# A fifteenth slab slot in a GNN and mixture kernel, and a rule in place of a table for the slot of each mixture load

## What is computed

```python
x = x + gnn_l(layernorm(x))        # attention over the edges, one or two layers, l = 0..3
x = x + ffn_l(layernorm(x))        # l = 0: attention and a small MLP, l = 2: 8 small experts
# l = 1 and l = 3: a mixture of 8 experts, 2 of them chosen for each row
out = sum over experts e of c[:, e] * ((silu(x @ Wg[e].T) * (x @ Wu[e].T)) @ Wd[e].T)
```

## Time and profile before

| | us |
|---|---|
| median of three runs | 1215.71 (1215.35 to 1215.76) |
| the profiled execution, its own time | 1215.62 |
| its span, first to last instruction | 1213.8 |
| PE busy | 1147.2 (95%) |
| VectorE busy | 564.9 (47%) |
| ScalarE busy | 446.8 (37%) |
| data moved | 443.13 MB, mean 365 GB/s |

### The profile page before, as it was taken

The page is one execution under the profiler, slowest core; times in us unless marked ns, Lnnn a source line. Parts: engine busy times, 40 slices in busy tenths (PEclk is TensorE's granted clock), DMA queues, the critical chain, the costliest instruction groups (busy, mean ns, idle before and its releaser), DMA issues.

```text
span 1213.8 us, 15596 instructions
## 1 busy us (share of the span) xinstructions
PE 1147.2 (95%) x6307; PEld 717.6 (59%) x6307; DVE 564.9 (47%) x880; ACT 446.8 (37%) x516; POOL 21.9 (2%) x47
## 2 busy tenths in 40 slices
PE   5899999989999999989999999999999999889978
PEld 4677785656855455535866686565665555445533
DVE  6977732437644234301665684454554533233310
ACT  4766512224633233201444364343544422222210
POOL 2000000000000000000000000000000000000000
PEclk9999999999999999999999999999999999899999
DMA  9998555945999999999567498999999999999996
GB/s 371 423 374 339 218 221 211 422 169 229 386 419 425 424 426 426 424 421 417 222 234 268 192 390 327 426 425 425 425 427 424 426 424 425 426 425 425 426 423 273
DMA packets 45222, 443.13 MB, mean 365 GB/s; under 512 B 5072, under 2 KB 5232, under 8 KB 11872
## 3 DMA queue, kind: packets, MB, share of 16 engines
q1 hardware_dynamic: 42336, 427.05, 85.0%
q0 software_dynamic: 2816, 15.09, 3.2%
HBM read 441.73 MB, written 0.39 MB: 364 GB/s over the span
## 4 chain that ended last, share of the span: by engine, by line
PE 75%; DMA 14%; DVE 6%; ACT 4%; issue 1%; SPq 0%; POOL 0%; DVEq 0%; ACTq 0%
PE PJ L1896 15%; PE PJ L1865 10%; PE TP L1955 8%; DMA scratch<-in_weights 7%; PE AC L1933 7%; DMA ring<-in_weights 6%; PE PJ L1874 5%; PE AC L1681 3%; PE AC L1693 3%; PE PJ L1856 2%; PE TP L1906 2%; PE MS L1528 2%; PE PJ L1641 1%; PE TP L1824 1%; DVE extra L1058 1%
## 5 line engine op out<-in xcount | busy, mean ns | idle before, releaser
L1896 PE MATMUL PJ<-scratch,picked 128*64 128x512 f32 (+1 forms) x564 | 145.9, 600 | 3.8 <-DMA scratch<-in_weights 3.8
L1955 PE MATMUL TP<-ring,extra 128*64 128x512 f32 (+3 forms) x720 | 118.0, 488 | 3.5 <-issue 3.5
L851 ACT ACTIVATE low<-PJ 128x512 f32<-128x512 f32 x51 | 30.3, 593 | 231.5 <-PE PJ L1896 158.9
L1292 DVE SCALAR_TENSOR_TENSOR act<-low,CB,PJ 128x512 f32<-128x512 f32 x51 | 38.0, 745 | 164.2 <-PE PJ L1865 84.1
L1310 DVE TENSOR_TENSOR ring_lo<-ring,w_hi_u 128x1536 fp32r<-128x1536 f32 x46 | 79.6, 1756 | 69.7 <-ACT w_hi_u L868 69.6
L1896 PE MATMUL PJ<-ring,picked 128*32 128x512 f32 (+1 forms) x456 | 101.6, 594 | 0.0
L868 ACT ACTIVATE w_hi_u<-ring 128x1536 fp32r<-128x1536 f32 x46 | 67.0, 1485 | 57.2 <-PE AC L1933 26.9
L1310 DVE TENSOR_TENSOR ring_lo<-ring,w_lo_u 128x1536 fp32r<-128x1536 f32 x40 | 68.9, 1755 | 37.9 <-ACT w_lo_u L868 37.8
L1955 PEld LDWEIGHTS TP<-ring,extra 128*64 128x64 f32 (+1 forms) x720 | 47.1, 126 | 63.0 <-issue 54.7
L1874 PE MATMUL PJ<-ring_lo,XTh 128*128 128x512 f32 x198 | 79.0, 399 | 0.0
L1896 PEld LDWEIGHTS PJ<-scratch,picked 128*64 128x64 f32 (+1 forms) x564 | 42.4, 126 | 60.4 <-issue 59.7
(11 more groups left out here) (439 smaller groups left out, 2099.6 us busy)
## 6 DMA issues: line engine op xcount, KB each, us to landing
ring<-in_weights SPq DMA_DIRECT2D x158, 1536.0 KB, 17.8
scratch<-in_weights SPq DMA_DIRECT2D x78, 1536.0 KB, 20.7
extra<-in_weights SPq DMA_DIRECT2D x23, 1536.0 KB, 20.7
extra<-in_attn POOLq DMA_DIRECT2D x11, 768.0 KB, 9.8
ring<-in_weights SPq DMA_DIRECT2D x10, 768.0 KB, 29.9
scratch<-in_weights SPq DMA_DIRECT2D x12, 384.0 KB, 16.6
extra<-in_attn POOLq DMA_DIRECT2D x6, 512.0 KB, 9.7
extra<-in_weights SPq DMA_DIRECT2D x4, 768.0 KB, 26.0
```

What stands on the lines that cost most here:

```text
L851: A(silu, PJ[:, 0:SEG], ACT.Silu).then_inc(S("silu_ready"), 1)
L1292: v.scalar_tensor_tensor(hexp, silu, weight, PJ[:, SEG:2 * SEG], ALU.mult, ALU.mult) \
L1896: ins = mm(dst[c], x[:, t, c], slab_at(LOAD[q, kind, side])[:, t * SEG:(t + 1) * SEG], start=(t == 0), stop=(t == KT - 1))
L1955: ins = mm(Y[c, a:b], hT_of(q)[:, t * P:(t + 1) * P][:, c], slab_at(LOAD[q, "d", side])[:, t * D + a:t * D + b], start=(j == j0 and t == 0 ...
```

## The change

A fifteenth slot, number 14, is added as a fourth plane of `extra`. Its 12,288 bytes in every partition come from the scratch of POOL's DMA descriptors, for which the program now asks 2048 bytes (before it asked for nothing, and the library's default is 16,384). The two tables go. `uses_of` lists the order in which a mixture's products run, and `slots_in_turn` gives each load the slot whose slab has the earliest last use; the tokens' slot 13 enters that list with the place at which the tokens are used up, and slot 12 is not used behind load 70 of the first mixture. The first mixture so has 13 slots, the second 12, and nine slots take slabs 117 to 126. The small tiles of the GNNs of layers 1 and 3 are laid closer together, inside slot 6 alone, so that slot 7 is free for its first mixture load at an earlier event.

```diff
-TURN = {
-    1: [0, 1, 8, 9, 2, 3, 4, 13, 5, 7, 12, 6],
-    3: [8, 9, 2, 3, 4, 5, 0, 1, 7, 12, 6],
-}
-OPENING = {
-    1: [0, 1, 8, 9, 2, 3, 4, 5, 6, 7, 12],
-    3: [8, 9, 2, 3, 4, 5, 0, 1, 6, 7, 12],
-}
...
-free = [SLOT[n] for n in range(L2_SLAB - len(TURN[1]), L2_SLAB) if SLOT[n] in QUIET]
+RING_SLOTS, SPLIT_SLOTS = range(0, 6), range(6, 12)
+EXTRA_AT = {12: 0, 13: 1, 14: 3}
+N_SLOTS = 15
+QUIET = [0, 1, 2, 3, 4, 5, 8, 9, 14]
+TOKENS_SLOT = 13
+VECTORS_SLOT, VECTORS_SLOT_UNTIL = 12, 70
+
+def uses_of(l):
+
+    first, end = MOE[l]["first"], LAST_PASS[l] + 1
+    order = [(kind, p) for q in range(first, end + 1) for kind, p in (("g", q), ("u", q), ("d", q - 1))]
+    return {(p, kind, side): at for at, (kind, p) in enumerate(order) if first <= p < end for side in range(sides(p))}
+
+def slots_in_turn(l, opening):
+
+    uses = uses_of(l)
+    given_up = {s: k - len(opening) for k, s in enumerate(opening)}
+    if l == 1:
+        given_up[TOKENS_SLOT] = uses[MOE[1]["first"] + 1, "d", 0] + 0.5
+    taken = []
+    for k, load in enumerate(loads_of(l)):
+        s = min((s for s in given_up if s != VECTORS_SLOT or l != 1 or k < VECTORS_SLOT_UNTIL), key=given_up.get)
+        given_up[s] = uses[load]
+        taken.append(s)
+    return taken
+
+SLOT = {n: n % RING for n in range(MOE[1]["slab"])}
+for k, s in enumerate(slots_in_turn(1, [14, 7, 0, 1, 8, 9, 2, 3, 4, 6, 5, 12])):
+    SLOT[MOE[1]["slab"] + k] = s
...
 for k in range(10):
-    SLOT[L2_SLAB + k] = free[k % 8]
+    SLOT[L2_SLAB + k] = free[k % 9]
+for k, s in enumerate(slots_in_turn(3, [7, *free[1:8], 6, free[8], free[0], 12])):
+    SLOT[MOE[3]["slab"] + k] = s
...
-        with nc.sbuf_tensor("extra", [P, 3, SLAB], F32) as extra:
+        with nc.sbuf_tensor("extra", [P, 4, SLAB], F32) as extra:
...
-                        if SLOT[n] in (6, 7):
+                        if SLOT[n] == 6:
                             sp.wait_ge(S("segment_product"), segments)
+                        if SLOT[n] == 7:
+                            sp.wait_ge(S("context" if l == 1 else "x_product"), {1: 1, 3: 4}[l])
...
-    nc = bacc.Bacc("TRN2", target_bir_lowering=False, num_devices=1)
+    nc = bacc.Bacc("TRN2", target_bir_lowering=False, num_devices=1, dynamic_dma_scratch_size=2048)
```

More of the change, by code:

```diff
@@ L140 @@
         LOAD[load] = MOE[l]["slab"] + k
-RING_SLOTS, SPLIT_SLOTS, EXTRA_SLOTS = range(0, 6), range(6, 12), range(12, 14)
-HI_SLOTS = (10, 11)
-TURN = {
-    1: [0, 1, 8, 9, 2, 3, 4, 13, 5, 7, 12, 6],
-    3: [8, 9, 2, 3, 4, 5, 0, 1, 7, 12, 6],
-}
-OPENING = {
-    1: [0, 1, 8, 9, 2, 3, 4, 5, 6, 7, 12],
-    3: [8, 9, 2, 3, 4, 5, 0, 1, 6, 7, 12],
-}
[L155 to L168, removed]
-free = [SLOT[n] for n in range(L2_SLAB - len(TURN[1]), L2_SLAB) if SLOT[n] in QUIET]
+RING_SLOTS, SPLIT_SLOTS = range(0, 6), range(6, 12)
[22 more added lines that the diff above has]
+    SLOT[MOE[1]["slab"] + k] = s
+free = []
+for n in range(L2_SLAB - 1, MOE[1]["slab"], -1):
+    if SLOT[n] in QUIET and SLOT[n] not in free:
+        free.insert(0, SLOT[n])
 for k in range(10):
-    SLOT[L2_SLAB + k] = free[k % 8]
+    SLOT[L2_SLAB + k] = free[k % 9]
+for k, s in enumerate(slots_in_turn(3, [7, *free[1:8], 6, free[8], free[0], 12])):
+    SLOT[MOE[3]["slab"] + k] = s
 HI = {}
@@ L299, in gnn_ffn_kernel @@
         ring_lo = sb("ring_lo", [P, RING, SLAB], F32R)
-        with nc.sbuf_tensor("extra", [P, 3, SLAB], F32) as extra:
+        with nc.sbuf_tensor("extra", [P, 4, SLAB], F32) as extra:
             pass
-        extra_lo = sb("extra_lo", [P, 3, SLAB], F32R)
+        extra_lo = sb("extra_lo", [P, 4, SLAB], F32R)
         at = [0]
@@ L396, in gnn_ffn_kernel @@
         ALT = carve(3 * SEG)
+        narrow = {
+            2: (hs1[:, 0:2 * SEG], hs1[:, 2 * SEG:4 * SEG], hs1[:, 4 * SEG:6 * SEG]),
+            5: (hs1[:, 0:4 * SEG], hs1[:, 4 * SEG:4 * SEG + 3 * P], hs1[:, 4 * SEG + 3 * P:4 * SEG + 6 * P]),
+        }
         end[0] = H_RING * SEG
@@ L441, in slab_at @@
                 return scratch[:, (s - RING) * SLAB:(s - RING + 1) * SLAB]
-            return extra[:, s - 2 * RING, :]
+            return extra[:, EXTRA_AT[s], :]
         def slab_lo(n):
@@ L450, in slab_lo @@
                 return (wh if s % 2 == 0 else wl)["dgu"[(s - RING) // 2]][:]
-            return extra_lo[:, s - 2 * RING, :]
+            return extra_lo[:, EXTRA_AT[s], :]
         def graph_hi(s, half):
@@ L481, in gnn_ffn_kernel @@
         Y = TP[:, SEG:SEG + D]
-        land = [S(f"slab_landed_{i}") for i in range(14)]
+        land = [S(f"slab_landed_{i}") for i in range(N_SLOTS)]
         def landed(eng, n):
@@ L502, in group, with group_at, h_tile @@
             n = min(k, GAT[c]["H"] - g * k)
-            at = (g % 3) * SEG
+            at = group_at(c, g)
             return GROUP_BASE[c] + g, n, slice(at, at + n * P)
+        def group_at(c, g):
+            return (g % 3) * (P if c == 5 else SEG)
+        def h_tile(c, j):
+            return narrow[c][0][:, j * SEG:(j + 1) * SEG] if c in narrow else hs1[:, ring_seg(j)]
         def logit_tile(c):
-            return low[0] if c in LAYER2_BIAS else EE
+            return low[0] if c in LAYER2_BIAS else narrow[c][1] if c in narrow else EE
         def attn_tile(c):
-            return low[1] if c in LAYER2_BIAS else ALT
+            return low[1] if c in LAYER2_BIAS else narrow[c][2] if c in narrow else ALT
         def rows_tile(c, g):
@@ L719, in copy_h @@
                 act.wait_ge(S(name), value)
-                A(hs1[:, ring_seg(j)], bank(j), ACT.Copy).then_inc(S("h_copied"), 1)
+                A(h_tile(c, j), bank(j), ACT.Copy).then_inc(S("h_copied"), 1)
             def copy_h2():
@@ L1232, in first_narrow @@
                         dve.wait_ge(S("h_copied"), SEG_BASE[c] + t + 1)
-                        terms(GAT[c]["unit"] + t, range(t * k, t * k + k), C, hs1[:, ring_seg(t)])
+                        terms(GAT[c]["unit"] + t, range(t * k, t * k + k), C, h_tile(c, t))
                         if c == 5 and t == 0:
@@ L1638, in attend @@
                     g = h // GAT[c]["group"]
-                    a = (g % 3) * SEG + (h % GAT[c]["group"]) * P
+                    a = group_at(c, g) + (h % GAT[c]["group"]) * P
                     o = at - i * SEG
-                    ins = mm(bank(i)[:, o:o + end - at], ALT[:, a:a + P],
-                             hs1[:, (i % H_RING) * SEG + o:(i % H_RING) * SEG + o + end - at],
+                    ins = mm(bank(i)[:, o:o + end - at], attn_tile(c)[:, a:a + P], h_tile(c, i)[:, o:o + end - at],
                              start=False, stop=(end == (i + 1) * SEG), skip_group_check=True)
```

## The result

The changed kernel takes **1208.45 us** (median of 4 runs, 1207.72 to 1209.44) beside 1215.74 us before (1215.35 to 1216.71). The ratio is 0.994 [0.9927, 0.9953]: 7.3 us less, with an interval of 5.7 to 8.9 us. Timed again on two chips, beside the kernel before on each, it gave 0.9947 [0.993, 0.9965] and 0.9943 [0.9925, 0.9961]. The forecast was 1209.3 us, faster.

What follows compares the result with a forecast made beforehand. Both mixtures were taken as races of the load queue, at 3.70 us a slab. Gains of 2.7 us in the first and 3.7 us in the second made 6.4 us, forecasting 1209.3 us, range 1207.0 to 1212.0 us.

Steps and rivals of the forecast that it cites:

- Term 1: First mixture, 320 to 324 us: loading slabs ahead of the tokens' wait closes the queue's hole, 2.7 us (0 to 3.7).
- behind 345 us the queue is full already: First mixture: the reason given why the added slot brings nothing there beyond the hole's 2.7 us.
- Term 2: Second mixture: one slot more gives one slab's lead at the last dry release, 747.84 us, worth 3.7 us (0 to 5.0).
- from there on the queue is full in both kernels: Second mixture, behind the release at 747.84 us: the lead of one slab, 3.7 us, is kept to the end.
- Sum: Whole kernel: 2.7 + 3.7 = 6.4 us off the profiled 1215.62 us, giving a median of 1209.3 us.
- Passing on: Between the mixtures: the first's 2.7 us arrive whole at the second's first routed load, 690.35 us moving to about 687.7.
- PE's idle time at the two ends: Ends of both mixtures: a sign that PE's idle time shrinks by about 3 and 4 us.
- Loads at nothing, and the scratch at nothing: Loads needing no routing and POOL's smaller descriptor scratch cost nothing; at worst one slab, 3.7 us, and 9.8 us respectively.
- the holes did not close altogether: Rival, both mixtures: releases come earlier too and all holes close, 13.4 us, 1202.3 us; chance 0.05, with any gain over 9 us.
- neither gain came alone: Rival, both mixtures: only one of the two gains comes, 1212.0 or 1213.0 us; chance 0.08.
- the slot was not spent ahead of the gate: Rival: the fifteenth slot takes a slab needing no routing and buys nothing behind it, 1215.7 us; chance of no effect 0.06.
- `rstd` came at 5.39 us: Rival at POOL's start: short scratch holds its second vector load 9.8 us, `rstd` later than 6 us, 1219.1 us; chance 0.05.

Runs made afterwards that it cites:

- the order alone: The changed kernel with slot 14 unused in both mixtures, so fourteen slots in the give-up order, timed against the kernel before: 1216.14 us, ratio 1.0001.
- the slot without the order: The changed kernel with its fifteen slots going round in a fixed circle instead of the give-up order, timed against the kernel before: 1217.79 us, ratio 1.002.
- one pass more ahead: The changed kernel with AHEAD 4 instead of 3, so twelve slabs of the second mixture need no routing: 1210.99 us, 0.996 against the kernel before.
- the scratch alone: The kernel before with only POOL's descriptor scratch cut from 16,384 to 2048 bytes: 1215.69 us, ratio 0.9996.

## Why the prediction was right, and where its terms were off

- **What bounds the kernel**: right. Both mixtures are races of the queue; what the queue gains behind its last dry moment arrives at the end. The time from end 1 to gate 2 has no trend with the change (125.2 to 129.2 us over all kernels), so the gain is passed on.
- **Term 1, the hole of the first mixture, 2.7 us (0 to 3.7)**: mis-sized. It measured 4.1 us (277.5 to 273.4, the means of the kernels with fourteen slots and of those with the slot here), a little over the upper bound. Two steps failed. The term was put down to the order of the waits, the slot being said to add nothing in the first mixture: the kernel with the order alone gains nothing that the timing shows, the slot without the order nothing either. It takes both, and together they give the lead that the argument reserved for the second mixture. And the step "behind 345 us the queue is full already" left the stretch from 324 to 345 us unread. Between 330 and 345 us the kernel before runs at 411 GB/s and loses another 0.5 us, so 3.2 us with the hole. The last 1.0 us is not in the data moved: by the mean of its sixteen marks the mixture's last strip comes 3.1 us earlier, and the last mark then stands 1.3 us behind that mean instead of 2.2 (five profiles of each kind, with the closing strips as in the changed kernel). That the marks lie closer together with the slot is shown, its cause is not. The same is seen in landings: slabs 53 and 54 lie 5.7 us apart before and 3.7 after, and from 54 to 62 it takes 31.9 us before and 29.6 after, 2.0 + 2.3 us.
- **Term 2, a slab's lead in the second mixture, 3.7 us (0 to 5.0)**: right in its mechanism, and 0.6 us too large: 3.1 us from gate 2 to slab 264 (493.0 to 489.9, means over the kernels with fourteen slots or with the circle, and over those with slot 14 here; the kernel with one pass more ahead is left out). The step that failed is "from there on the queue is full in both kernels": the 8 us behind the dry stretch run at 378 GB/s instead of 413 and give 0.7 us back. The rest of the dry stretch stayed, as stated: 352 GB/s. The 1.3 us that were counted as lost from 690.5 to 716 us, and put into the upper bound, are mostly the time from the first issue to its first data: from 691.44 to 716.94 us the same kernel moves 415 GB/s.
- **Sum**: 4.1 + 3.1 = 7.2 us against the 6.4 predicted and the 7.3 [5.7, 8.9] measured. That the sum came out so near is partly luck, since the two errors lean against each other. The profiled execution shows only 6.2 us: its closing strips took 1.5 us longer and gate 1 came 0.4 us later, and 0.8 us came back behind the last landing.
- **Passing on**: gate 2 was put at 687.7 us and came at 686.41, mostly by term 1's error.
- **PE's idle time at the two ends**, put at 3 and 4 us less: 63.00 - 58.61 = 4.4 us in the 63 us up to the end of the first mixture (the stretch 496.50 to 559.50; 8.4 before), so 4.0 less; 306.00 - 289.42 = 16.6 us in the second (18.7 before), 2.1 less.
- **Loads at nothing, and the scratch at nothing**: right. The first routed load of the first mixture went 0.36 us later in the first profile (285.98 us) and at 285.65 and 285.59 us in the other two, and the scratch alone is at 0.9996. SP's queue is no shorter with the small scratch: before and with the scratch alone, every load of SP whose issue takes over 1.2 us finds nine to twelve loads in flight. The Trainium skill (DMA: Bandwidth & Descriptors, SWDGE vs HWDGE vs iDMA), by which the prediction weighed this, says that descriptors of SP's loads are made by hardware, and these figures agree; no run here shows the rings themselves.
- **Rivals**: the holes did not close altogether; neither gain came alone; the slot was not spent ahead of the gate; `rstd` came at 5.39 us.

## What to carry to other kernels

Where a stream of loads waits for room in a ring of buffers, look for the last moment at which it does. In this kernel a buffer more was worth about one transfer there (4.1 and 3.1 us; a transfer is 3.7 us), however full or empty the stream was elsewhere, and filling idle time ahead of that moment only moved the idle time. The buffer paid only where the transfer that takes it waits for the product that comes first: a load that waits for a later one holds everything behind it in an in-order queue, and a fixed circle with one buffer more gained nothing (1.002). When a hole is to be closed, read the stretch behind it too: closing it by order alone moved it some 10 us on, and behind the second mixture's dry stretch part of the lead was lost again.

## What the runs showed of the hardware that was not expected

An issue of SP takes 0.33 us as a rule, and up to 7.37 us in the changed kernel with nine or more loads in flight (the step on SP's line of strips in the chain above), so near the end SP's issues themselves appear on the chain. A load's sixteen landing marks do not come together: those of slab 62 spread over 3.0 us before and 1.9 us after, and the products wait for the last. And the last strips do not run at the queue's pace: in the profiled execution of the changed kernel the last 10 us before the last landing at 1201.0 us are these:

```profile
1190.00:1195.00 5.00, 4.49 (x28) 1.83 (x28) 0.00 (x0) 0.60 (x1) 0.00 (x0) 1.00 0.94 368
1195.00:1200.00 5.00, 4.64 (x28) 1.73 (x26) 0.00 (x0) 0.00 (x0) 0.00 (x0) 1.00 0.26 102
```

The mean share of the 16 DMA engines falls to 0.26 while the last strips are still on their way; the last strip's first mark comes 5.1 us ahead of its last.
